# First stage of a decoder kernel: f32 projection replaced by three f16 products, position sums moved behind the gates' products

## What is computed

```python
xn = layer_norm(x, in_ln_w, in_ln_b)
proj = xn @ W_in.T + b_in                       # 256 -> 4*512 + 16
q, k, v, p, y = split(proj, [512, 1024, 1536, 2048])
smear = sigmoid(smear_factor)                   # per head, 16 heads of 32
k = (1 - smear) * k + smear * k_prev            # k_prev: k one token earlier
pos = cumsum(sigmoid(y), over tokens)
mask = causal - (pos_i - pos_j)
attn = softmax(q/s @ (k/s).T / sqrt(32) + mask)
out = silu(p) * (attn @ v) @ W_out.T            # then layer norm, residual, layer norm
```

## Time and profile before

| | us |
|---|---|
| median of three runs | 3297.32 |
| profiled execution, its time | 3301.9 |
| profiled execution, its span | 3300.1 |
| first stage up to its barrier (l0p) | about 169 |
| PE busy in the span | 2515.7 (76%) |
| DVE busy | 1860.6 (56%) |
| ACT busy | 1433.0 (43%) |
| mean granted PE clock | 0.880 |

### The profile page before, as it was taken

The page is one execution under the profiler, slowest core; times in us unless marked ns, Lnnn a source line. Parts: engine busy times, 40 slices in busy tenths (PEclk is TensorE's granted clock), DMA queues, the critical chain, the costliest instruction groups (busy, mean ns, idle before and its releaser), DMA issues. The chain is left out here.

```text
span 3300.1 us, 43983 instructions
## 1 busy us (share of the span) xinstructions
PE 2515.7 (76%) x15362; PEld 1403.3 (43%) x15362; DVE 1860.6 (56%) x5005; ACT 1433.0 (43%) x2891; POOL 978.5 (30%) x802
## 2 busy tenths in 40 slices
PE   6978886696535778888885669887776788858977
PEld 3323333465422323333353255555444333346666
DVE  4476664566658655555523548334442577746678
ACT  4324442364321256666621514213511355537876
POOL 1045552136456366666612300000101110101300
PEclk9979998798877889999987879998687799978999
DMA  3211111530354321111001210111000422114023
GB/s 110 73 41 42 42 22 30 167 108 28 113 179 88 92 57 45 36 39 45 16 14 59 41 39 1 55 58 33 15 0 15 90 28 28 15 48 121 2 77 103
DMA packets 185739, 182.86 MB, mean 55 GB/s; under 512 B 55161, under 2 KB 152186, under 8 KB 184750
## 3 DMA queue, kind: packets, MB, share of 16 engines
q1 hardware_dynamic: 176110, 167.48, 17.9%
q0 software_dynamic: 9408, 12.56, 2.4%
HBM read 121.81 MB, written 61.59 MB: 56 GB/s over the span
## 5 line engine op out<-in xcount | busy, mean ns | idle before, releaser
L941 POOL TENSOR_TENSOR l1a_p_lo<-res,l1a_p_hi 128x1024 f16<-128x1024 f32 x192 | 311.7, 1641 | 177.6 <-ACT res L1182 177.6
L1191 ACT ACTIVATE l0a_probs<-ps 128x1024 f32<-128x1024 f32 (+1 forms) x192 | 145.6, 810 | 175.4 <-PE ps L1045 103.3
L1191 ACT ACTIVATE l3a_probs<-ps 128x1024 f32<-128x1024 f32 (+1 forms) x192 | 146.7, 808 | 142.0 <-PE ps L1045 114.9
L1181 ACT ACTIVATE l1a_p_hi<-ps 128x1024 f16<-128x1024 f32 x192 | 157.9, 823 | 113.5 <-PE ps L1045 83.5
L1042 PE MATMUL ps<-l1a_qs,l1a_ks 128*128 128x512 f16 (+3 forms) x768 | 166.9, 332 | 32.2 <-ACT res L1182 32.2
L1213 DVE CUSTOM_DVE_ANT_0 l1a_masked<-ps,l1a_wide_mask 128x128 bf16<-128x128 f32 (+3 forms) x256 | 117.9, 489 | 102.6 <-PE ps L1011 100.3
L1011 PE MATMUL ps<-l1a_ks,l1a_qs 128*128 128x512 f16 (+3 forms) x384 | 121.2, 344 | 62.3 <-DVE l1a_nmax L1216 33.1
L966 POOL TENSOR_TENSOR l0a_both<-l0a_probs 128x768 f32<-128x768 f32 (+2 forms) x96 | 154.5, 1631 | 46.3 <-PE ps L1083 46.1
L1182 ACT ACTIVATE res<-ps 128x1024 f32<-128x1024 f32 x192 | 158.5, 825 | 0.0
L1045 PE MATMUL ps<-mask_t,ident_b 128*128 128x128 bf16 x768 | 157.2, 225 | 0.0
L1213 DVE CUSTOM_DVE_ANT_0 l0a_masked<-ps,l0a_wide_mask 128x128 bf16<-128x128 f32 (+3 forms) x256 | 116.4, 488 | 67.7 <-PE ps L1011 67.0
(11 more groups left out here) (732 smaller groups left out, 6419.4 us busy)
## 6 DMA issues: line engine op xcount, KB each, us to landing
f_wf<-in_L_ffn_w_dram SPq DMA_DIRECT2D x16, 1024.0 KB
f_slots<-x0a_zeros SPq DMA_DIRECT2D x32, 256.0 KB, 3.5
f_xe<-f_slots SPq DMA_DIRECT2D x32, 256.0 KB, 2.9
f_ys<-f_y SPq DMA_DIRECT2D x32, 256.0 KB
l1a_qs<-l_q_h SPq DMA_DIRECT2D x64, 128.0 KB
d_wall<-in_L_ffn_W_dram SPq DMA_DIRECT2D x3, 2112.0 KB
l0a_qs<-l_q_h SPq DMA_DIRECT2D x32, 128.0 KB
l0a_ks<-l_k_h SPq DMA_DIRECT2D x16, 256.0 KB
```

The source lines that it names most:

```text
L941: pool.tensor_tensor(ph_lo[:, n % SLOTS, :, 0:w], probs[:, n % FULL, :, 0:w], ph_hi[:, n % SLOTS, :, 0:w], ALU.subtract).then_inc(s_["low_ ...
L1181: act.activation(ph_hi[:, n % SLOTS, :, 0:w], SB[n % 2][:, :, 0:w], ACT.Exp)
L1191: act.activation(probs[0:KR, n % SLOTS, 2 * pr:2 * pr + 2, 0:w], SB[x % 2][:, :, 0:w], ACT.Exp).then_inc(s_["exps"], 1)
```

## The change

It has three parts. (1) The weights are split into two f16 tiles, high by ACT (four copies) and low by DVE (four subtractions), and the normalized columns likewise through `parts`. (2) Every product of q, k, gates and v is three f16 products (high x high, high x low, low x high) instead of one f32 product; y stays f32. (3) DVE's program is reordered: the low halves of q and the whole of k come first, then the scan and the parts of the positions, then v. The f32 input rows and columns go to `xr` and `xtr`, which makes room for the f16 tiles.

```diff
-    xin = ph.sb("n_xin", [P, NG, GT, D]) if x_in is not None else k.xr.rearrange("p (g t) d -> p g t d", t=GT)
+    xin = k.xr.rearrange("p (g t) d -> p g t d", t=GT)
...
-            xnt = ph.sb("xnt", [P, DC, N])
+            xnt = k.xtr
+            xp = [ph.sb(f"x{i}", [P, DC, N], F16) for i in range(2)]
+            wp = [ph.sb(f"w{i}", [P, DC, 4 * E], F16) for i in range(2)]
+            TERMS = [(0, 0), (0, 1), (1, 0)]
+            steps = [(d, m, x) for d in range(DC) for m, x in TERMS]
...
-                norm_program(ph, block, x_in, xnt, a["L0_attn_in_ln_w"], a["L0_attn_in_ln_b"], [k.ps[:, 4:6, :], k.ps[:, 6:8, :]])
+                norm_program(ph, block, x_in, xnt, a["L0_attn_in_ln_w"], a["L0_attn_in_ln_b"], [k.ps[:, 4:6, :], k.ps[:, 6:8, :]], parts=xp)
+
+                def chunk(t, i):
+                    return t[:, :, i * E:(i + 1) * E]
...
+                            if b == 0 and c == 0:
+                                pe.wait_ge(ph.s["n_lower"], NG)
+                            if b == 0 and c % EC == 0:
+                                pe.wait_ge(ph.s["w_lo"], c // EC + 1)
                             for half in range(2):
-                                for d in range(DC):
-                                    ins = pe.matmul(PA[c % 2][:, half * 512:(half + 1) * 512], w[:, d, c * P:(c + 1) * P],
-                                                    xnt[:, d, b * T + half * 512:b * T + (half + 1) * 512], start=d == 0, stop=d == DC - 1)
+                                for n, (d, m, x) in enumerate(steps):
+                                    ins = pe.matmul(PA[c % 2][:, half * 512:(half + 1) * 512], wp[m][:, d, c * P:(c + 1) * P],
+                                                    xp[x][:, d, b * T + half * 512:b * T + (half + 1) * 512], start=n == 0, stop=n == len(steps) - 1)
...
+                            if b == 0 and c == 0:
+                                pe.wait_ge(ph.s["w_lo"], 3)
...
-                            for d in range(DC):
-                                ins = pe.matmul(PV[j % 2], xnt[:, d, b * T + j * P:b * T + (j + 1) * P], w[:, d, 2 * E:3 * E], start=d == 0, stop=d == DC - 1)
+                            if b == 0 and j == 0:
+                                pe.wait_ge(ph.s["w_lo"], 4)
+                            for n, (d, m, x) in enumerate(steps):
+                                ins = pe.matmul(PV[j % 2], xp[x][:, d, b * T + j * P:b * T + (j + 1) * P], wp[m][:, d, 2 * E:3 * E], start=n == 0, stop=n == len(steps) - 1)
...
                     act.wait_ge(ph.s["w_ld"], 80)
-
+                    for i in (0, 1, 3, 2):
+                        act.activation(chunk(wp[0], i), chunk(w, i), ACT.Copy).then_inc(ph.s["w_hi"], 1)
                     act.activation(sg[:, 0, :], hf[:, 0, :], ACT.Sigmoid).then_inc(ph.s["act_prep"], 1)
...
+                    def lower_weights(n, i):
+                        dve.wait_ge(ph.s["w_hi"], n + 1)
+                        dve.tensor_tensor(chunk(wp[1], i), chunk(w, i), chunk(wp[0], i), ALU.subtract).then_inc(ph.s["w_lo"], 1)
+
+                    lower_weights(0, 0)
+                    lower_weights(1, 1)
                     dve.wait_ge(ph.s["act_prep"], 2)
...
                     for b in range(B):
                         done = b * DONE
+                        for c in range(EC):
+
+                            dve.wait_ge(ph.s["act_q"], b * EC + c + 1)
+                            dve.wait_ge(ph.s["q_hi"], b * EC + c + 1)
+                            dve.tensor_tensor(los[:, c % 2, :], st[:, c % 2, :], his[:, c % 2, :], ALU.subtract).then_inc(ph.s["lo_done"], 1)
+                            if b == 0 and c < 2:
+                                lower_weights(2 + c, 3 - c)
+                        for c in range(EC):
+                            dve.wait_ge(ph.s["kraw_ready"], b * EC + c + 1)
...
                         dve.wait_ge(ph.s["sig_ready"], b + 1)
 
                         dve.tensor_tensor_scan(pos[:], ones[:], sig[:], 0.0, ALU.mult, ALU.add).then_inc(ph.s["pos_ready"], 1)
...
                         parts.close()
-                        for c in range(EC):
-
-                            dve.wait_ge(ph.s["act_q"], b * EC + c + 1)
...
```

More of the change, by code:

```diff
@@ L1574, in _ @@
                                 after(pe, ph.s["gate_ready"], b * EC + c - 1)
+                            if b == 0 and c == 0:
+                                pe.wait_ge(ph.s["w_lo"], 3)
                             for half in range(2):
-                                for d in range(DC):
-                                    ins = pe.matmul(PA[c % 2][:, half * 512:(half + 1) * 512], w[:, d, 3 * E + c * P:3 * E + (c + 1) * P],
-                                                    xnt[:, d, b * T + half * 512:b * T + (half + 1) * 512], start=d == 0, stop=d == DC - 1)
+                                for n, (d, m, x) in enumerate(steps):
+                                    ins = pe.matmul(PA[c % 2][:, half * 512:(half + 1) * 512], wp[m][:, d, 3 * E + c * P:3 * E + (c + 1) * P],
+                                                    xp[x][:, d, b * T + half * 512:b * T + (half + 1) * 512], start=n == 0, stop=n == len(steps) - 1)
                             ins.then_inc(ph.s["pe_done"], 1)
@@ L1632, in _ @@
                         done = b * DONE
+                        for c in range(EC):
[6 more added lines that the diff above has]
+                            dve.wait_ge(ph.s["kraw_ready"], b * EC + c + 1)
+                            after(dve, ph.s["lo_done"], b * CH + EC + c - 1)
+                            s = st[:, c % 2, :]
+                            dve.tensor_scalar(s, kraw[:], sg[:, 4, c:c + 1], None, ALU.mult).then_inc(ph.s["smear"], 1)
+                            dve.wait_ge(ph.s["smear"], b * EC + c + 1)
+                            dve.scalar_tensor_tensor(out=st[:, c % 2, 1:T], in0=kraw[:, 0:T - 1], scalar=sg[:, 0, c:c + 1],
+                                                     in1=st[:, c % 2, 1:T], op0=ALU.mult, op1=ALU.add).then_inc(ph.s["k_ready"], 1)
+                            dve.wait_ge(ph.s["k_hi"], b * EC + c + 1)
+                            dve.tensor_tensor(los[:, c % 2, :], st[:, c % 2, :], his[:, c % 2, :], ALU.subtract).then_inc(ph.s["lo_done"], 1)
                         dve.wait_ge(ph.s["sig_ready"], b + 1)
```

2 lines of the change are left out of this document (1 added, 1 removed).

## The result

The changed kernel takes 3274.31 us (median of 8 runs) against 3305.12 for the kernel before (8 runs): the ratio is **0.9929, 95% interval 0.9905 to 0.9953**. The profiled execution after took 3290.18 (span 3288.4, mean clock 0.877), only 11.7 less than the one before. Executions of the same kernel differ by this much, so the change is measured where it lies: by the start of the attention's first product behind the stage's barrier. It came at 168.96 before and comes at 146.81 now, **22.15 us earlier**. Behind it the profiled execution after took 10.5 us longer than the one before.

A forecast was written before the change was run, and what follows sets the result against it. PE bounds the last gates and v, ACT's store waits q, the kraw loop k. Terms -3.8 - 5.3 + 3.0 - 5.5 - 5.3 + 3.0 = -13.9 us, from the 3297.3 median, give 3283.4 us; range 3272 to 3293.

The forecast's parts named there:

- A: Whole kernel: the forecast itself, with a clock fall at the gates' gap in each batch, 3283.4 us; chance 0.50.
- rival B: Gap ahead of the third gate chunk: the clock holds there, 6.0 us less, total 3277.4; chance 0.20.
- The price of a product: Last two gates and v: an f16 product of 512 columns takes 0.215 us, saving 5.3 us a batch.
- K: k stretch: faster products bring nothing, 0 us, since the loop through the single kraw tile sets the pace.
- The cover of the scan: Scan moved behind k: cover of 7.7 us against 7.84 us of scan and parts, so 0 us.
- The opening: Start of batch 0 up to q's first high half: 5.1 us later, at 40.9 against 35.75.
- The release by q's stores: q: 4.75 us from the end of the low half to ACT's third high half, at 49.2 in batch 0.
- The clock at the gates: Gap ahead of the third gate chunk grows to 2.9 to 3.1 us; clock falls, +3.0 us a batch.
- C: q of batch 0: gains nothing because the longer opening eats it, 3.8 us more, total 3287.2; chance 0.16.
- D: Last gates and v: clock stays at 0.50 once fallen, +9.9 us a batch, total 3307.8; chance 0.06.
- E: Last gates and v: products overlap more, evictions bound, -13.1 us a batch, total about 3262; chance 0.02.
- F: Behind the stage's barrier: what the stage saves is lost there, total 3297; chance 0.06.

The follow-up runs named there:

- the shortened opening: Changed kernel with ACT's four weight copies spread, only the first ahead of the small vectors: 3277.31 us in one execution.
- filled or used gaps: Changed kernel with eight unread products behind the second gate chunk, 3272.55 us; or with two v tiles there, 0.9927, and also two kraw tiles, 0.9884.

## Why the prediction was right in direction and short in size

The time of 3274.31 lies in the stated range of 3272 to 3293, 2.3 us above its lower end. The direction was right, and so were most of the terms; but the sum lacked 8.3 of 22.15 us, and four shortfalls all point one way. A's own 3283.4 less the 5 us left for the runs' spread would not have reached 3274.31; the time is in the range because rival B's 3277.4 and the same 5 us stretch it downwards. That is partly luck.

**The price of a product: right.** 0.215 us was forecast, and 48 v products take 10.52 us with their last tail. The saving of 5.3 us a batch appears whole in batch 0 (5.16). The 131 ns of the Trainium skill's page "TensorE: Matmul & The Clock Gate", section "Back-to-back issue gap", are not borne out by the changed kernel either.

**K: right.** 0.0 and +0.27, the latter in batch 1, where k's second chunk on PE met a fall (granted clock 0.73 from 107.80 to 113.80); the single kraw tile set the pace (4.33 us). Two tiles brought it to 3.32.

**The cover of the scan: right.** It was forecast level, and it is. In batch 0 no v eviction waits for it.

**The opening: right, 0.85 us too long.** The first high half came at 40.05, not 40.9.

**The release by q's stores: the step that failed.** I wrote "From the second store's issue to ACT's release the rows give 4.3 to 5.0 us (the lower in batch 1 ...; the higher in batch 0 with the position stores beside it). I take 4.75". Both rows had position stores beside them, since DVE made the positions first in both batches, so neither end showed the release without them. Measured: 2.87 and 3.15 us. This moved the third high half by 1.9 us in batch 0 (the opening moved it by 0.85 more), and it is 1.6 of the 1.7 us missing in batch 1. I had noted that the position stores move with the scan, and looked only for what they might hit at their new place, not for what they set free at the old one. Removing them alone (-8.8 us) and putting their like back (2.5 us more in batch 1) settles it.

**PE in q of batch 0: a second step that failed, hidden by luck.** I had PE begin q at 33.3, stand from 38.7 to 43.2 and carry the half clock through chunks 2 and 3, so that the first kraw came at 54.4. (PE may start chunk c once `st` of chunk c-2 is written, as the prediction has it, and not c-1, as the description of the kernel says.) The timeline of PE shows no such gap and no fall, and the window over chunks 2 and 3 has a granted clock of 1.00:

```profile
36.47 5.35 PE L1578 MATMUL ps<-l0p_x,l0p_w 128*128 128x512 f16 x24
42.38 5.35 PE L1578 MATMUL ps<-l0p_x,l0p_w 128*128 128x512 f16 x24 [0.56 <-ACT l0p_st L1622]
```

```profile
42.40:47.70 5.30, 5.30 (x24) 1.00 0.40 150
```

The gap had shrunk because the y product ahead of q took 6.57 us instead of 3.6, which the forecast did not have. An estimate of what the forecast fall would have done: from 42.4, three chunks of 2.58 and 3.0 us lost give a first kraw near 53.2 instead of 51.62. The opening and the release alone would then have brought only some 1.2 of the 2.8 us missing in batch 0, and the other 1.6 are owed to the fall that did not come. In the kernel with early v tiles a smaller fall at this place (60 products in 14.81 us instead of about 13.0) put the first kraw 0.4 later than in the second profile of the changed kernel.

**The clock at the gates: the mechanism right, the price too high and not certain.** The gap was 2.90, as forecast (2.9 to 3.1). I took 6 us at 0.50, worth 3.0. The two stretches of that length stand behind gaps of 5.39 and 3.40 us; behind 2.90 the whole pair of chunks takes 1.3 to 1.7 us longer. And the fall does not always come. Over the profiles here:

| gap ahead of the third gate chunk | pairs of chunks | clock fell |
|---|---|---|
| 2.90 us | 12 | 10 |
| 1.96 or 1.97 us | 6 | 1 |
| 0.31 to 1.60 us | 6 | 0 |

The first row holds the changed kernel twice, the products alone, both kernels with added stores and the shortened opening; the second the kernel before, DVE's order alone and the later position stores; the third the three with filled or used gaps. The run with two thirds of q's and k's products left out isn't counted, since PE did less before the gap: there the clock fell behind 2.45 and 2.90 us. The length of the gap alone doesn't decide at other places either: in q the clock stayed at 1.00 behind 2.93 us (later position stores, 49.10 to 55.10) and fell behind 1.96 us (early v tiles). The forecast's +6.0 was +1.7 in the profile after, all in batch 1. The Trainium skill's section "HAM oscillation — how this bites in real kernels", on the same page, describes such a loss where waits come again and again, and as to its kind the traces agree. But its rule for how long a wait does no harm lets 2.90 us pass, so by that rule rival B stood and A was out; the 10 falls in 12 are against it. What a fall cost here is the 1.3 to 1.7 us above. Of the rivals, A is what occurs most often and B what batch 0 of the profile after showed.

**The rivals.** C fell: the first kraw gained 6.59. D fell: the clock was back at 0.99 within 3.8 us. E fell with the spacing, F with the timed runs (the ratio's 0.7% is 23 us, and the stage gained 22.15).

Summed, the 8.3 us that the forecast lacks are 2.8 and 1.7 in q, 2.9 and 1.1 at the gates, less 0.3 in k. What varies in the totals lies behind the stage: over the thirteen profiled executions here that part took 3117.7 to 3142.3 us, and PE's same 15058 instructions in it 2366.2 to 2394.2 us of busy time. That these are falls of the clock as in the first stage fits, but was not traced to its places.

## What to carry to other kernels

When a step is moved, list what its transfers shared a time with at the old place, too: a landing time read from the trace holds only with the neighbours that it had there. A price for a wait has to be taken from a row in which the neighbour is absent, or carry a bound for it. When products get cheaper, the gaps ahead of them grow; fill them with work that is ready (here v tiles between gates), which took away both the gap and the fall of the clock.

## What was unexpected of the hardware

- Two stores of 96 KB from 16 partitions took some 265 (an estimate, from SP's queue) to 307 ns a packet (GpSimd's), against 78 ns for stores of the same row length from 128 partitions, and made stores beside them land 0.9 to 2.5 us later.
- The same program, with the same gap of 2.90 us, had its clock fall in one batch and not in the other; once in six it fell behind 1.96 us ahead of the third gate chunk.
- The y product of batch 0 (f32, 16 columns of weights) took 6.57 us in the profile after instead of 3.6, and 5.2 to 6.5 in its variants, hidden under the copies of weights. Most of its instructions stand 0.85 us apart instead of 0.43, as they would at half clock, but the granted clock of the window reads 1.00, so the cause isn't shown:

```profile
29.96 6.57 PE L1561 MATMUL ps<-res,l0p_w 128*16 128x512 f32 x8 [1.63 <-ACT res L292]
```

```profile
29.96:36.50 6.54, 6.54 (x9) 1.00 0.00 0
```
